# Adding the second layer's bias to the fetched row instead of to the product, in a gated cross-attention block with routed experts

## What is computed

```
x   = x + tanh(g_xattn) * attention(layernorm(x), ctx)
xf  = layernorm(x)
idx = argmax(softmax(xf @ Wg + bg))
h   = gelu(xf @ W1[idx] + b1[idx])
out = x + tanh(g_ffn) * (h @ W2[idx] + b2[idx])
```

## Time and profile before

| | us |
|---|---|
| median of 3 runs | 317.39 |
| lowest and highest | 316.21, 318.24 |
| the profiled execution | 320.28 |
| its span, first to last instruction | 318.3 |
| TensorE busy (matmuls) | 287.7 |
| VectorE busy | 230.0 |
| GpSimd busy | 123.3 |
| ScalarE busy | 84.1 |

### The profile page before, as it was taken

The page is one execution under the profiler, slowest core; times in us unless marked ns, Lnnn a source line. Parts: engine busy times, 40 slices in busy tenths (PEclk is TensorE's granted clock), DMA queues, the critical chain, the costliest instruction groups (busy, mean ns, idle before and its releaser), DMA issues.

```text
span 318.3 us, 10091 instructions
## 1 busy us (share of the span) xinstructions
PE 287.7 (90%) x3173; PEld 219.7 (69%) x3174; DVE 230.0 (72%) x810; ACT 84.1 (26%) x219; POOL 123.3 (39%) x125
## 2 busy tenths in 40 slices
PE   8989999999899999999999997687889998899870
PEld 7557767577577676776776775466778787889760
DVE  7558678797788888798887977867786664655550
ACT  1011320321312302303213213123434444454420
POOL 8502022442423523524424433432364444344441
PEclk9999999999999999999999999979999999999995
DMA  8575346466465565564455123277467887677610
GB/s 266 171 192 151 93 111 189 102 211 197 129 203 153 167 206 136 184 204 109 130 152 150 46 69 84 80 197 194 147 191 231 233 258 215 194 241 231 190 52 0
DMA packets 35482, 51.40 MB, mean 161 GB/s; under 512 B 8189, under 2 KB 18558, under 8 KB 35456
## 3 DMA queue, kind: packets, MB, share of 16 engines
q1 hardware_dynamic: 20240, 25.69, 30.7%
q10 hardware_dynamic: 11808, 16.81, 16.8%
q0 software_dynamic: 3408, 8.59, 7.6%
HBM read 32.99 MB, written 10.60 MB: 137 GB/s over the span
## 4 chain that ended last, share of the span: by engine, by line
PE 59%; issue 10%; DVE 10%; DMA 7%; ACTq 4%; POOL 3%; ACT 2%; another core or an unknown queue 1%; DVEq 1%; POOLq 0%
PE ps_pr L393 11%; PE ps_qo L401 11%; PE ps_av L439 5%; PE ps_tr L557 5%; PE ps_so L557 5%; PE ps_to L571 5%; PE ps_av L571 5%; PE ps_so L419 4%; DMA routed_rows<-sb_xs,sb_pos_i 4%; DMA sb_x<-x_in 3%; PE ps_pr L547 2%; POOL sb_cn L279 2%; PE ps_av L512 2%; PE ps_tr L428 1%; DVE sb_om L794 1%
## 5 line engine op out<-in xcount | busy, mean ns | idle before, releaser
L393 PE MATMUL ps_pr<-sb_wkv,sb_ct 128*128 128x512 f32 x128 | 63.0, 616 | 0.5 <-DVE sb_y_v L749 0.5
L279 POOL TENSOR_TENSOR sb_cn<-sb_om,sb_rt 128x512 f32<-128x512 f32 x15 | 19.3, 1287 | 68.5 <-DVE sb_om L794 68.5
L627 ACT ACTIVATE sb_pe_x<-sb_pe_x 128x512 f32<-128x512 f32 x16 | 10.1, 631 | 124.6 <-DVE sb_pe_x L770 108.2
L1213 POOL DMA_INDIRECT routed_rows<-sb_xs,sb_pos_i x32 | 32.2, 1006 | 21.0 <-DVE sb_pos_i L885 10.5
L393 PEld LDWEIGHTS ps_pr<-sb_wkv,sb_ct 128*128 128x128 f32 x128 | 22.3, 191 | 20.0 <-issue 19.8
L401 PE MATMUL ps_qo<-sb_wog,sb_ot 128*128 128x264 f32 x128 | 32.9, 402 | 1.3 <-ACT sb_q_n L622 1.1
L439 PE MATMUL ps_av<-sb_vb,sb_at 128*32 128x128 f32 x1024 | 32.6, 274 | 0.9 <-issue 0.9
L401 PEld LDWEIGHTS ps_qo<-sb_wog,sb_ot 128*128 128x128 f32 x128 | 25.2, 199 | 11.4 <-issue 7.3
L439 PEld LDWEIGHTS ps_av<-sb_vb,sb_at 128*32 128x32 f32 x1024 | 27.4, 110 | 7.1 <-issue 7.1
L419 PE MATMUL ps_so<-sb_kb,sb_y_q 128*32 128x128 f32 x1024 | 31.1, 273 | 0.5 <-DVE sb_y_q L755 0.5
L401 PE MATMUL ps_qo<-sb_wqg_c,sb_xt 128*128 128x264 f32 x128 | 31.1, 386 | 0.0
(11 more groups left out here) (129 smaller groups left out, 490.1 us busy)
## 6 DMA issues: line engine op xcount, KB each, us to landing
sb_w<-w_in_ SPq DMA_DIRECT2D x24, 257.0 KB, 3.2
sb_xb<-routed_rows SPq DMA_DIRECT2D x39, 134.0 KB
sb_kb<-sb_y_k SPq DMA_DIRECT2D x124, 32.0 KB
sb_vb<-sb_y_v SPq DMA_DIRECT2D x124, 32.0 KB
sb_w<-w_in_ ACTq DMA_DIRECT2D x15, 257.0 KB, 3.4
sb_ct<-ctx_in ACTq DMA_DIRECT2D x15, 256.0 KB, 3.2
sb_x<-x_in ACTq DMA_DIRECT2D x15, 256.0 KB, 5.6
sb_xt<-xt_in_ ACTq DMA_DIRECT2D x14, 256.0 KB, 4.1
```

Source lines behind the costliest of these rows:

```text
L279: eng.tensor_tensor(cn[:].rearrange("p u h i -> p h u i"), om[:].rearrange("p h (u i) -> p h u i", u=2), rt[:].rearrange("p (u i) -> p u i ...
L393: last = pe.matmul(pr[:, s * 512:(s + 1) * 512], lhsT=ct[i][:, kc, s, :], rhs=wkv[:, kc, :], start=(kc == 0), stop=(kc == KC - 1))
L627: act.activation(pe_x[:], pe_x[:], ACT.Exp, scale=float(H) ** -0.5).then_inc(exp_done, 1)
L1213: pool.indirect_dma_start(rows, bass.IndirectOffsetOnAxis(ap=pos_i[:, s:s + 1], axis=0), xs[:, s, :], None).then_inc(routed, 16)
```

## The change

The bias table is multiplied once by the gate, in place, on ScalarE, at the end of slot 12 (of 0 to 15). A new VectorE step, add_bias, adds the scaled bias to `xb` in place, after the block has been normalised. finish then computes the output row straight from PSUM; its register load moves to add_bias, and the token numbers are computed ahead of the wait for the product. In VectorE's expert slot b, add_bias of block b+2 stands behind finish of block b-1. Blocks 0 and 1 get their bias at the head of the bridge, block 2 behind the statistics of pair 15. TensorE's layer 2 waits for the finished row (yf_done) instead of the bias addition.

```diff
             def layer2(b, i):
                 ex = pe.value_load(tab[0:1, 1, bass.ds(b, 1)], min_val=0, max_val=E - 1)
                 pe.wait_ge(gelu_done, b + 1)
-                wait(pe, yb_done, b - 1)
+                wait(pe, yf_done, b - 1)
...
                 if has(k, 1):
                     scale_q(k + 1)
+                if isinstance(k, int) and k == last_pair - 3:
+                    act.wait_ge(late_in, 16 * E)
+                    act.wait_ge(tanh_ok, 1)
+                    act.activation(b2_sb[:], b2_sb[:], ACT.Copy, scale=tg[:, 1:2]).then_inc(b2_scaled, 1)
...
+            def add_bias(b, q):
+
+                ex = dve.value_load(tab[0:1, 1, bass.ds(b, 1)], min_val=0, max_val=E - 1)
+                dve.wait_ge(xbn_done, b + 1)
+                dve.tensor_tensor(xb[q][:, 0:D], xb[q][:, 0:D],
+                                  b2_sb[:, bass.ds(ex, 1), :].rearrange("p a d -> p (a d)"), ALU.add).then_inc(with_bias, 1)
+
             def finish(b, q, nth):
 
                 i, j = q % 2, q % OUT
-                ex = dve.value_load(tab[0:1, 1, bass.ds(b, 1)], min_val=0, max_val=E - 1)
+                wait(dve, stored[j], 16 * nth)
+                dve.tensor_tensor(tok_i[j][:], xb[q][:, TOK:TOK + 1], skip[:, bass.ds(b, 1)], ALU.add)
+                dve.wait_ge(with_bias, b + 1)
                 dve.wait_ge(y_done, b + 1)
-                wait(dve, stored[j], 16 * nth)
-                dve.tensor_tensor(yo[i][:], y_ps[i],
-                                  b2_sb[:, bass.ds(ex, 1), :].rearrange("p a d -> p (a d)"), ALU.add).then_inc(yb_done, 1)
-                dve.tensor_tensor(tok_i[j][:], xb[q][:, TOK:TOK + 1], skip[:, bass.ds(b, 1)], ALU.add)
-                dve.wait_ge(yb_done, b + 1)
-                dve.scalar_tensor_tensor(yf[j], yo[i][:], tg[:, 1:2], xb[q][:, 0:D], ALU.mult, ALU.add).then_inc(yf_done, 1)
+                dve.scalar_tensor_tensor(yf[j], y_ps[i], tg[:, 1:2], xb[q][:, 0:D], ALU.mult, ALU.add).then_inc(yf_done, 1)
...
                 if not known or b > 0:
                     finish(b - 1, (q - 1) % RING, RING // OUT * turn + (q - 1) // OUT)
-
-
-            dve.wait_ge(late_in, 16 * E)
+                if not known or b + 2 < blocks:
+                    add_bias(b + 2, (q + 2) % RING)
+
+
+            dve.wait_ge(b2_scaled, 1)
+            for b in range(2):
+                add_bias(b, b)
             n = last_pair - 1
             pick_4(n)
             norm_b(2, 2, 0)
...
             stats_3(n, xs[n % 2])
+            add_bias(2, 2)
             expert_slot(1, 1, 0)
```

More of the change, by code:

```diff
@@ L181, in flamingo_block @@
         ht = [sb(f"ht_{i}", [P, KC, P]) for i in range(2)]
-        yo = [sb(f"yo_{i}", [P, D]) for i in range(2)]
         yf = [sb(f"yf_{i}", [P, D])[:] for i in range(2)] + [q_n[:, i, :] for i in range(2)]
@@ L239, in flamingo_block @@
         h_done, gelu_done = sem("h_done"), sem("gelu_done")
-        y_done, yb_done, yf_done = sem("y_done"), sem("yb_done"), sem("yf_done")
+        y_done, yf_done = sem("y_done"), sem("yf_done")
+        b2_scaled, with_bias = sem("b2_scaled"), sem("with_bias")
         stored = [sem(f"stored{i}") for i in range(OUT)]
```

## The result

The changed kernel takes 324.41 us in the median of 22 runs (318.93 to 327.93), the kernel before beside it 318.38 us (22 runs, 315.62 to 322.95). The ratio is 1.0122, 95% interval [1.0087, 1.0156]: **slower by 1.2%, some 3.9 us**. The comparison leaves disturbed runs out, so the ratio is not the quotient of the two medians (1.019). The forecast was +0.66 us, the range ended at 320.6.

The account below looks back on a forecast made before the run. The prediction took TensorE to bound the expert stage, at 1.98 us a block. Its terms 0 + 1.12 + 0 - 0.46 summed to +0.66 us, taking the median from 317.39 to 318.0 us; range 315.2 to 320.6.

Parts of the forecast that it names:

- Part 1: Slot 12: ScalarE's one multiplication of the bias table hides in idle time; 0 to 0.3 us, taken as 0.
- fourth rival: ScalarE's multiplication in slot 12 holds up its queue: +0.3 us on top, 318.3 us; chance 0.06.
- Part 2: Bridge head: two bias additions ahead of the ranks delay the output projection of pair 15 by 0.93 us.
- Part 3: Bridge: additions of blocks 2, 3 and 4 among its steps; delay carried through at +1.12 us.
- Part 4: Settled expert blocks: TensorE bounds them at 1.98 us each, VectorE's new order needs some 1.3; 0 us.
- 2.05 us as the sign of being wrong: Settled blocks: the forecast is wrong if blocks 20 to 35 take over 2.05 us each.
- the sentence on SyncE: Settled blocks: SyncE's fetch waits for a row ready 0.46 us earlier and is no bound.
- Part 5: Last block: the last store starts 0.46 us earlier (-0.46), limited by GpSimd and not by VectorE.
- VectorE becomes the bound of the blocks: Rival, slots from block 8: uncovered register loads make blocks 2.1 us; with the bridge 321.8 us; chance 0.12.
- Only the tail counts: Rival: an unnamed wait absorbs the bridge's delay, leaving 0.15 - 0.46 = -0.3, 317.1 us; chance 0.22.
- the unnamed wait: Late bridge, from 236.65: 1.78 us in the chain that the profile cannot name, possibly absorbing the delay.
- third rival: Late bridge gets shorter: unnamed stretches of 1.78 and 1.66 us vanish, with the tail 313.5 us; chance 0.10.

Follow-up runs that it names:

- e3: Kernel before plus only ScalarE's multiplication of the bias table by the gate; ratio 1.0020 to the kernel before.
- i2: Kernel before with SyncE's even-block weight fetches meant to be held until ScalarE's odd ones are issued; ratio 1.0020.
- f5: Kernel before plus dummy products filling TensorE's idle time in slot 15 and the bridge; ratio 0.9982.
- g4: Kernel before plus two additions with register loads at the head of VectorE's bridge, results never read; ratio 1.0080.
- f3: Kernel before with the new epilogue only for blocks 0 to 14, the other blocks finishing as before; ratio 0.9970.
- h2: Repeat of f3 (new epilogue for blocks 0 to 14 only), beside the whole change on one chip; ratio 0.9975.
- e2: Changed kernel without any bias addition, ScalarE's multiplication kept; ratio 1.0014 to the kernel before.
- f1: New epilogue only for blocks 15 to 38, blocks 0 to 14 finishing in two operations in the old form; ratio 1.0031 to the kernel before.
- i1: Changed kernel with SyncE's even-block weight fetches meant to be held until ScalarE's odd ones are issued; the edit missed; ratio 1.0056 to the kernel before.
- g1: Changed kernel measured again, unaltered, on another chip; ratio 1.0158 to the kernel before.
- g2: Changed kernel with ScalarE fetching the odd blocks' first-layer weights 5 blocks ahead instead of 3; ratio 0.9799 to the kernel before.
- h4: Repeat of g2 (changed kernel, odd weights 5 blocks ahead); ratio 0.9749 to the kernel before, median 308.89 us.
- h1: Changed kernel measured a third time, unaltered, on the same chip as h2; ratio 1.0124 to the kernel before.
- f7: Kernel before, old epilogue, with ScalarE fetching the odd blocks' first-layer weights 5 blocks ahead instead of 3; ratio 0.9741.
- h3: Repeat of f7 (kernel before, odd weights 5 blocks ahead); ratio 0.9794, median 310.17 us.

## Why the prediction was wrong

**Where the time goes, by the means of the profiles.** With three blocks of lead, S is 48.84 us in the mean of the seven kernels whose settled blocks have the old epilogue (before, e3, i2, f5, g4, f3, h2) and 50.74 in the eight with the new one: +1.9. I is 3.1 against 4.5 us, 1.4 of that difference, and D 3.72 against 4.14. B is 40.80 in the six without additions in the bridge (before, e3, i2, f5, e2, f1) and 42.84 in the nine with them: +2.0. T gives 0.9 back. Sum +3.0 us, 0.95%, against 1.2 to 1.6% measured. Without the five profiles that lie more than 1.5% above the fastest run of their kernel (after, e2, i1, g4, h2) the differences are +1.7 in S and +1.5 in B, and the sum is +2.2 us, 0.7%. The first sum, made with these same profiles, fits f1 (+1.9 - 0.9 = +1.0, 1.003; measured 1.0031), e2 (the same; 1.0014) and g4 (+2.0 - 0.4, 1.005; 1.0080). It fails for f3 and h2 (+1.7, 1.005; measured 0.9970 and 0.9975, twice). The single profiles of one kind spread from 46.94 to 50.80 us in S with the old epilogue and from 48.76 to 52.13 with the new, so differences of a third of a per cent carry no weight in this sum. Why the half with blocks 0 to 14 costs nothing stays open.

*Part 1, ScalarE's multiplication, 0.* Right: 2.01 us in idle time, x issued ahead of it, and alone (e3) no difference clear of noise. The fourth rival falls with it.

*Part 2, the two additions ahead of the ranks, +0.93 at the projection.* Right in kind, small in size: +1.16 in after, up to +1.36 in g1 (3.44 - 2.08). The term that was short is the second register load: I had let it run from the start of the first addition, with 0.60 us from one addition to the next, and it is 0.78 (219.75 to 220.53), 0.35 of it bare. The addition itself is 424 ns with both operands in SBUF, 425 out of PSUM; the equal pair that I took from the trace held. By the table of the Trainium skill (VectorE: DVE Perf Modes, "The TRN2 errata — SBUF-src ops pay a fixed extra latency per instruction"), which gives a PSUM source 62 cycles more, these two would differ by 65 ns, an estimate; the measurement decides against it here.

*Part 3, carried through the bridge at +1.12.* This term was too small too: the bridge came out at +2.0 in the mean and +3.65 in the one profile. In the profile of g4 a bare delay gives +2.3, and g2 and h4 point at what multiplies it: with the odd weights there in time, P is up by 1.36 and B by only 0.6 (39.59 against 38.97, means of two, which differ among themselves by up to 1.1). I had carried a delay along a chain in which I took every transfer as met. About 0.1 us was to stay of each load; it was 0.33.

*Part 4, the settled blocks, 0.* **The step that failed.** I wrote that the chain runs "block after block through TensorE alone" and took 1.98 us from the distance of two starts. Those two starts are an even and an odd block without a wait between them; the mean block of the same profile takes 2.24. Blocks 20 to 35, for which I had named 2.05 us as the sign of being wrong, take 2.30 already in the kernel before. 9.48 busy of 10 was half a microsecond of waiting in five blocks, 18.44 of 20 further on is half as much again over the same time, and that wait belonged to the odd weights. From there the sentence on SyncE, that a fetch 0.46 us earlier "is no bound", was asked the wrong way round. It is no bound for its own block. What an earlier issue does to a transfer that is bound was never asked. That the new epilogue lengthens the landing of the odd weights is a reading of D and O over fifteen profiles, with one exception (e3, old epilogue, D 4.11), and not shown by an experiment. The landings themselves go the same way: with the old epilogue in the settled blocks ScalarE's take 3.25 to 3.39 us in the median (f5, g4, f3, h2; 8 to 11 landings each), with the new one 3.77, 3.98 and 3.54 (f1, g1, h1; 11, 8 and 5), while SyncE's, which go first, stay at 2.95 to 3.05 in all seven. That the loss is gone when the landing has slack is shown (f7, h3 against g2, h4).

*Part 5, the tail, -0.46.* Right in sign, half the size: about -0.92 in every kernel with the new epilogue there. The scaled addition of block 37 starts 0.17 us behind the start of the last layer 2; in the old kernel the first operation of that finish started 0.58 behind it, from 307.49 to 308.07, and I had held that start fixed. Not all of it is the operation saved: T is already 4.13 to 4.15 in g4, f3 and h2, whose last blocks have the old finish.

*The rivals.* "VectorE becomes the bound of the blocks" named about the right size (321.8) with the wrong cause: VectorE's work is 230.2 us after and 230.0 before, and with weights in time its blocks run at TensorE's 1.96 us. "Only the tail counts" comes near to what happens with the lead of 5, though not through the unnamed wait, and is not what happens with the lead of 3. The unnamed wait of the third rival goes with the chip and not with the change (last section).

## What to carry to other kernels

Before a stage is called bound by an engine, take its mean over many blocks and compare it with the sum of that engine's work; here 92 to 95% busy, with a wait in every fourth block, was a transfer with too short a lead, whatever semaphore the bracket named. Then an edit elsewhere that shifts delays or transfers by a microsecond can come out as several. Here the lead was worth 2.1 to 2.6% where the epilogue was worth nothing: fetch 5 blocks ahead first, then judge the epilogue, which with that lead may be used either way (0.9741 and 0.9794 old, 0.9799 and 0.9749 new). That the prefetch whose data is wanted soonest should be issued first is a guess from D and O; the run that was to test it did not.

## What the runs showed of the hardware

ScalarE's 257 KB weight fetches landed in 3.2, 3.4 and 4.2 us in before, where the core moved 229 to 254 GB/s; in the settled blocks of the five kernels with the lead of 5, at 202 to 267 GB/s by stretches of 20 us, both queues' took 2.6 to 5.5 us. A product that had waited for such a landing started 0.09 us behind it. The loads of a register from SBUF stay bare by 0.33 to 0.36 us in front of the instruction that uses them even when the engine had 0.4 us of work in front of it. In the bridge ScalarE has one stall of some 3 us without a cause of its own, which is the third rival's wait:

```profile
239.76 0.37 ACT L707 COPY sb_ct<-ps_pr 128x256 f32<-128x256 f32 x1 [3.17 <-PE ps_pr L547]
```

It is there in all profiles of before and after at first and in all of the first and the fifth group, old and new epilogue alike (in the old ones in front of a gelu instead of this copy), and in none of the second, third and fourth group, which ran on other chips. The ratio of the changed kernel is the same with it and without (1.0122; 1.0158 and 1.0124). The Trainium skill (Runtime: NRT & Kernel Launch, "Instruction fetch mechanics") has instruction fetches mostly hidden; no run here shows whether this stall is one.
